# Attention on one core: the band mask added in PSUM by VectorE instead of by products on TensorE

## What is computed

```python
q, k, v = (layernorm(x) @ W.T + b for each of Wq, Wk, Wv)     # 16 heads of 32
scores = einsum("bhqd,bhkd->bhqk", q, k) * 32 ** -0.5
banned = (j >= 4) & (j < i - 128)                              # i: query, j: key
probs = softmax(where(banned, -inf, scores))
x = x + einsum("bhqk,bhkd->bhqd", probs, v) @ Wo.T + bo
```

## Time and profile before

| | us |
|---|---|
| median of 3 runs (lowest, highest) | 792.04 (791.56, 792.66) |
| span of the profiled execution, first to last instruction | 789.9 |
| PE busy in the span | 735.5 (93%) |
| DVE busy | 597.9 (76%) |
| ACT busy | 471.4 (60%) |
| POOL busy | 333.0 (42%) |
| mean granted TensorE clock | 0.976 |

### The profile page before, as it was taken

The page is one execution under the profiler, slowest core; times in us unless marked ns, Lnnn a source line. Parts: engine busy times, 40 slices in busy tenths (PEclk is TensorE's granted clock), DMA queues, the critical chain, the costliest instruction groups (busy, mean ns, idle before and its releaser), DMA issues. The chain is left out here.

```text
span 789.9 us, 14108 instructions
## 1 busy us (share of the span) xinstructions
PE 735.5 (93%) x5130; PEld 509.0 (64%) x5130; DVE 597.9 (76%) x1102; ACT 471.4 (60%) x1024; POOL 333.0 (42%) x330
## 2 busy tenths in 40 slices
PE   5988999999999999999987959999998999999984
PEld 4766777777777777777755747888874444444431
DVE  6886766886668866766677547887888999999982
ACT  5555766666667666766555214444455777667761
POOL 2011204213142134454373343445546667777662
PEclk9999999999999999999997979999999999999998
DMA  9200021304030331215330075455430233333231
GB/s 319 108 1 28 27 66 70 108 28 161 28 108 28 108 134 54 81 55 189 107 108 1 2 252 198 176 194 202 149 120 31 53 82 94 88 99 97 77 80 54
DMA packets 55218, 78.33 MB, mean 99 GB/s; under 512 B 36335, under 2 KB 38383, under 8 KB 53424
## 3 DMA queue, kind: packets, MB, share of 16 engines
q1 hardware_dynamic: 46336, 51.99, 20.2%
q0 software_dynamic: 8528, 24.93, 9.1%
q10 hardware_dynamic: 288, 0.52, 0.2%
HBM read 56.92 MB, written 17.59 MB: 94 GB/s over the span
## 5 line engine op out<-in xcount | busy, mean ns | idle before, releaser
L556 ACT ACTIVATE probs<-s_ps,neg_max 128x512 f32<-128x512 f32 (+2 forms) x256 | 152.3, 610 | 20.3 <-DVE neg_max L725 18.6
L725 DVE TENSOR_REDUCE neg_max<-s_ps 128x2 f32<-128x1024 f32 (+2 forms) x128 | 124.5, 1014 | 33.1 <-PE s_ps L963 32.6
L983 PE MATMUL pT_ps<-ident,probs 128*128 128x128 f32 x832 | 116.6, 282 | 9.3 <-DVE probs L746 8.3
L568 ACT ACTIVATE probs<-pT_ps 128x512 f32<-128x512 f32 x96 | 57.4, 598 | 98.6 <-PE pT_ps L983 97.8
L983 PEld LDWEIGHTS pT_ps<-ident,probs 128*128 128x128 f32 x832 | 95.0, 145 | 24.7 <-DVE probs L746 11.0
L746 DVE COPY probs<-pT_ps 128x512 f32<-128x512 f32 x112 | 76.8, 685 | 36.8 <-PE pT_ps L983 36.8
L1681 POOL TENSOR_TENSOR xg_own<-h,ln_w_sb 128x512 f32<-128x512 f32 x64 | 83.9, 1322 | 33.9 <-DVE h L1767 33.8
L896 PE MATMUL side_ps<-w_hi 128*128 128x512 f32 x172 | 71.1, 414 | 0.0
L420 POOL TENSOR_TENSOR aT_hi<-norm,one_col 128x512 fp32r<-128x512 f32 x15 | 15.6, 1040 | 125.4 <-DVE norm L737 87.1
L896 PE MATMUL side_ps<-w_hi,w_lo 128*128 128x512 f32 x172 | 67.5, 392 | 0.0
L896 PE MATMUL side_ps<-w_lo,w_hi 128*128 128x512 f32 x172 | 67.1, 390 | 0.0
(11 more groups left out here) (285 smaller groups left out, 1800.1 us busy)
## 6 DMA issues: line engine op xcount, KB each, us to landing
w_piece<-w_ffn SPq DMA_DIRECT2D x24, 512.0 KB, 3.5
w_stage<-w_ffn SPq DMA_DIRECT2D x12, 1024.0 KB, 4.8
xres<-x POOLq DMA_DIRECT2D x4, 1024.0 KB, 5.7
xn<-x SPq DMA_DIRECT2D x3, 1024.0 KB, 8.5
x<-xres POOLq DMA_DIRECT2D x3, 1024.0 KB, 4.8
xn<-c SPq DMA_DIRECT2D x2, 1024.0 KB, 6.1
v_next<-c SPq DMA_DIRECT2D x2, 1024.0 KB, 7.9
xn<-x SPq DMA_DIRECT2D x4, 256.0 KB, 3.5
```

The source lines that it names most:

```text
L556: nc.scalar.activation(weights[qt][:, h, at:at + width(qt)], s_ps[:, h, 0:width(qt)], ACT.Exp, bias=neg_max[:, qt % 2, h:h + 1], accum_out ...
L568: nc.scalar.activation(out, turned_p, ACT.Identity).then_inc(slot_copied[0], 1)
L725: nc.vector.tensor_reduce(neg_max[:, qt % 2, 2 * s:2 * s + 2], s_ps[:, 2 * s:2 * s + 2, 0:width(qt)], AX.X, ALU.max, negate=True).then_inc ...
L983: last = nc.tensor.transpose(pT_ps[:, k % 2, h * P:h * P + P], weights[qt][:, h, a:z], ident[:])
```

## The change

The four mask products of a masked unit are gone from PE. VectorE adds the same `window_mask` in place to the scores in PSUM, in one instruction for two heads (2 x 128 columns, or 2 x 124 for qt = 1), directly ahead of the maximum over these two heads, and waits for its own result (`masked_scores`) before it takes the maximum. `scores_ready` is now counted with the last score product of every second head, in all units. The clearing of `v_sinks` counts in `consts_ready` too, which now goes to 9; PE, the load of the sinks on SP, and VectorE ahead of its first maximum wait for 9.

```diff
--- before.py
+++ after.py
@@ -163,7 +163,7 @@
         rstd_ready, xn_ready = sem("rstd_ready"), sem("xn_ready")
         side_done, side_hi, side_left = sem("side_done"), sem("side_hi"), sem("side_left")
         sinks_gathered = sem("sinks_gathered")
-        v_sinks_cleared, v_sinks_loaded = sem("v_sinks_cleared"), sem("v_sinks_loaded")
+        v_sinks_loaded = sem("v_sinks_loaded")
         v_moved, c_split, rows_clipped = sem("v_moved"), sem("c_split"), sem("rows_clipped")
         c_loaded = [sem(f"c_loaded{n}") for n in range(EXPERTS)]
         piece_loaded, piece_done = sem("piece_loaded"), sem("piece_done")
@@ -171,6 +171,7 @@
         list_cleared, list_written, list_loaded = sem("list_cleared"), sem("list_written"), sem("list_loaded")
         dense_written, dense_loaded, x2_filled = sem("dense_written"), sem("dense_loaded"), sem("x2_filled")
         scores_ready, max_ready, exp_done = sem("scores_ready"), sem("max_ready"), sem("exp_done")
+        masked_scores = sem("masked_scores")
         slot_transposed, slot_copied = sem("slot_transposed"), [sem("slot_copied_act"), sem("slot_copied_dve")]
         heads_done, rinv_ready, rinv_widened = sem("heads_done"), sem("rinv_ready"), sem("rinv_widened")
         attn_ready, attn_hi_ready, attn_split = sem("attn_ready"), sem("attn_hi_ready"), sem("attn_split")
@@ -215,6 +216,9 @@
 
         def units_before(b, g, qt):
             return b * GU + g * TT + qt
+
+        def masks_before(b, g, qt):
+            return (b * HG + g) * (TT - 1) + qt - 1
 
 
 
@@ -349,7 +353,7 @@
                 load_piece(0, 0)
                 sp.wait_ge(side_left, nth(-1, "X3"))
                 load_x(1)
-                sp.wait_ge(v_sinks_cleared, 1)
+                sp.wait_ge(consts_ready, 9)
                 sp.wait_ge(side_left, nth(-1, "V0"))
                 place_sinks()
                 for b in range(BATCH - 1):
@@ -376,8 +380,8 @@
                 nc.gpsimd.memset(window_mask[:], 0.0).then_inc(consts_ready, 1)
                 nc.gpsimd.memset(minus_half[:], -0.5).then_inc(consts_ready, 1)
                 nc.gpsimd.memset(one_col[:], 1.0).then_inc(consts_ready, 1)
-                nc.gpsimd.memset(v_sinks[:], 0.0).then_inc(v_sinks_cleared, 1)
-                pool.wait_ge(consts_ready, 5)
+                nc.gpsimd.memset(v_sinks[:], 0.0).then_inc(consts_ready, 1)
+                pool.wait_ge(consts_ready, 6)
                 for t in (ident, ident_bf):
                     nc.gpsimd.affine_select(out=t[:], in_=t[:], compare_op=ALU.not_equal, fill=1.0, base=0,
                                             pattern=[[-1, P]], channel_multiplier=1).then_inc(consts_ready, 1)
@@ -722,6 +726,13 @@
 
                 def maxima(b, g, qt, s):
                     dve.wait_ge(scores_ready, units_before(b, g, qt) * 2 + s + 1)
+                    if blocks(qt)[2]:
+                        at = SINKS if qt == TT - 1 else 0
+                        free = SINKS if qt == 1 else 0
+                        scored = s_ps[:, 2 * s:2 * s + 2, at + free:at + P]
+                        nc.vector.tensor_tensor(scored, scored, window_mask[:, free:P].unsqueeze(1).to_broadcast([P, 2, P - free]),
+                                                ALU.add).then_inc(masked_scores, 1)
+                        dve.wait_ge(masked_scores, 2 * masks_before(b, g, qt) + s + 1)
                     nc.vector.tensor_reduce(neg_max[:, qt % 2, 2 * s:2 * s + 2], s_ps[:, 2 * s:2 * s + 2, 0:width(qt)],
                                             AX.X, ALU.max, negate=True).then_inc(max_ready, 1)
 
@@ -850,6 +861,7 @@
                     then(nc.vector.tensor_scalar(dense_row[:], dense[:], P - 1, None, ALU.bitwise_and))
                     then(nc.vector.scalar_tensor_tensor(dense_at[:], dense_row[:], float(TILES), dense_tile[:], ALU.mult, ALU.add))
 
+                dve.wait_ge(consts_ready, 9)
                 maxima(0, 0, 0, 0)
                 maxima(0, 0, 0, 1)
                 dve.wait_ge(wide_bias_loaded, 32)
@@ -943,7 +955,6 @@
                         project(name, side_ps[:], whole).then_inc(side_done, 1)
 
                 def scores(b, g, qt):
-                    sink, kts, masked = blocks(qt)
                     if qt == 0:
                         pe.wait_ge(side_left, keys_projected(b, g))
                     if units_before(b, g, qt):
@@ -953,16 +964,9 @@
                         for h in range(GH):
                             rows = slice(HD * h, HD * h + HD)
                             last = nc.tensor.matmul(s_ps[:, h, 0:width(qt)], q[rows, g % HG, cols], key_columns(k, rows, g % HG, qt),
-                                                    start=(n == 0), stop=(n == 2 and not masked), tile_position=(HD * h, 0))
-                    if not masked:
-                        last.then_inc(scores_ready, 2)
-                        return
-                    at = SINKS if qt == TT - 1 else 0
-                    free = SINKS if qt == 1 else 0
-                    for h in range(GH):
-                        last = nc.tensor.matmul(s_ps[:, h, at + free:at + P], ident_bf[:], window_mask[:, free:P], start=False, stop=True)
-                        if h % 2:
-                            last.then_inc(scores_ready, 1)
+                                                    start=(n == 0), stop=(n == 2), tile_position=(HD * h, 0))
+                            if n == 2 and h % 2:
+                                last.then_inc(scores_ready, 1)
 
                 def transpose_slot(b, g, qt, k):
                     slot = slots_of(qt)[k]
@@ -1044,7 +1048,7 @@
                     if name:
                         side(b, nth(b, name), name)
 
-                pe.wait_ge(consts_ready, 8)
+                pe.wait_ge(consts_ready, 9)
                 for t in range(TT):
                     pe.wait_ge(xn_ready, t + 1)
                     transpose_x(t, s_ps[:, t, :]).then_inc(side_done, 1)
```

## The result

The changed kernel takes 804.46 us (median of 4 runs, 802.55 to 806.96), the one before beside it 791.8 (786.52 to 792.66). The ratio is 1.019 (95%: 1.0158 to 1.0222), so some 15 us slower, with 12.5 to 17.6 as the interval (the two medians themselves lie 12.7 apart). The forecast was 8.5 slower, 800.5 us; the result lies inside the range of 795.2 to 807.5. Timed again (6 runs), it has the same ratio. So the sign was right and about two fifths of the loss were missing from the sum.

A forecast was written before the change was run, and what follows sets the result against it. PE was taken to bound most of attention, DVE its start and end; by unit classes 2.2 + 2.3 + 2.2 + 5.9 + 0.0 - 4.1 = +8.5 us, on the 792.0 median 800.5 us, range 795.2 to 807.5.

The forecast's parts named there:

- What bounds the kernel, and where the change bites: Attention: PE bounds most, DVE start and end; DVE's added work delays the slot 1 copy that PE awaits.
- The price of the addition: On DVE: 0.42 to 0.43 us per addition, 0.90 us per unit with waits, 43 us in all.
- 0.20 each: Rival, faster: DVE additions cost 0.20 us each, giving -4 us, 788 us; chance 0.07.
- 0.60 each: Rival, dearer addition: reading and writing PSUM in place costs 0.6 us each, +17 us, 809 us; chance 0.12.
- the one without a price for the wait: Rival: a dependent maximum on DVE starts without delay, a unit costs 0.70 us, +3.5 us, 795.5 us; chance 0.10.
- (a): Six units like (1,3,0), qt = 0, rounds 1 and 3: slot 3 waits for DVE's copy; 0.36 us each, +2.2.
- (c): Five units with statistics of x ahead of the copy, like (0,4,1): twice +0.6, three times +0.3, +2.2 us.
- (b): Three units like (1,2,0): PE's transposes of x wait for DVE's later sum for v; +0.76 us each, +2.3.
- (f): Seventeen units like (1,3,2), where the copy has slack: PE's saving counts in full, 17 x -0.24 = -4.1 us.
- (e): Nine units at about zero, such as those like (1,3,1) and (1,4,0), where other waits absorb PE's saving: 0.0 us.
- The clock: Rival: PE waits bring half speed mid-phase, 8 us of it giving 4 us too little work, 804 us; chance 0.13.
- (d): Eight units already bound by DVE, at attention's start and end: +0.7 to +0.9 us, one pair 0.9 together; +5.9 us.

The follow-up runs named there:

- The kernel without masks: Changed kernel with neither mask products nor additions, so banned keys keep their scores; 784.57 us, ratio 0.9929.
- the kernel before with POOL's new order: Kernel before, with POOL's load_residual of batches 1 to 3 put behind the widening of round 1's reciprocals; 789.21 us, ratio 1.0001.
- the kernel with 16 additions: Masks added by DVE in 16 units (qt = 2 or 3), PE products in the other 32; 788.09 us; with load_residual behind the widening 786.27 us, ratio 0.9969.
- the kernel with idle products: Changed kernel with 6 or 8 extra unread PE products in each of the nine units without side work; 805.46 us, ratio 1.0207.

## Why the prediction was right, and where its sum fell short

*What bounds the kernel, and where the change bites*: right. PE's share between 100 and 200 us fell to 95.8% (forecast 95), the waits for the slot 1 copies there rose to 6.2 us (forecast 5 or more), and they lie in the units named. The expert phase starts 16.7 us later (2.2 of it from ahead of the first unit), where 8 to 9 was named as the sign.

*The price of the addition*: right, 425 and 419 ns for 0.42 to 0.43, and 0.92 for a unit's two with their waits for 0.90. (The two maxima of the earlier trace rows last 1.22 and 1.21 us, so they do overlap by the 0.08 that the prediction took; with the 1.20 that it wrote it would be 0.05.) The two rivals that turned on it (0.20 each, 0.60 each) fall, and so does the one without a price for the wait. On that last one the Trainium skill (VectorE: DVE Perf Modes, The DRAIN you can't avoid) says, of eight copies in a row, that the semaphores between them cost nothing extra. The trace differs: here the addition runs 230.71 to 231.13 and its maximum starts at 231.17; that pair and the next take 0.46 and 0.45 us more than a maximum alone, not 0.35.

*Classes (a) to (c)*: right, 7.0 for 6.7. (a) and (b) are right to 0.1 us; in (c) the two units with qt = 1 took 0.71 more each where 0.6 was forecast.

*Class (f)*, "seventeen units that save in full", -4.1: the term that was too large. Twelve units save 0.17 to 0.20, not 0.24, the same for a narrow gap as for a wide one. Those like (1,2,2) save 0.06 to 0.09, because PE's transposes of x wait there for v (0.24 us in (1,2,2) of the changed kernel). (e) and (f) without (0,0,0) and (0,1,2) come to -2.5. The kernel without masks has the same figures, so they are PE's.

*(1,1,3) and (2,1,3)*, +0.69 and +0.66: the step that was missing. The prediction has no term for POOL's queue. Its widening was the last to come there already, by 0.2 us, as the kernel before with POOL's new order shows, so PE's saving was not to be had in these units; and in (1,1,3) POOL waits 0.46 us longer for the store than before. That is 1.35 us for the two units. In the kernel with 16 additions such a loss goes with the new order; in the changed kernel itself PE's wait for the widening is read from the trace, and its cure was not tried.

*The clock*, a rival with 0.13 and 8 us at half clock for 4 us of time: it came **beside** the forecast case and not in its place. 13.7 us of 35 to 400 us were at half clock, against 3.4 in the profile that I read; the products that ran in it cost 3.4 us by the kernel with idle products. It didn't come in the middle of the phase, from waits of 0.3 us, as that rival had it, but where PE already waited 2.6 us and now waits 2.7. And it isn't the change's alone: all three profiles of the changed kernel have the 13.7, but the kernel before, with 3.4 in its first profile and in the one with POOL's new order, shows 10.2 us in its second, with (0,0,3) 1.5 us longer. In that second pair batch 0's first units lose 4.0 us and not 5.9, and (3,2,0) to (3,3,1) lose 5.8 and not 3.3: from 400 to 455 us the kernel before stood at half clock for 6.8 us there and for 13.7 in its first profile, the changed one for 13.7 in both pairs. Attention as a whole grows by the same 15 us. So how much of the loss is the clock's can't be said from one pair. The Trainium skill (TensorE: Matmul & The Clock Gate, HAM oscillation) warns that idle gaps take the clock down repeatedly. The trace agrees for the units bound by DVE, where the clock fell twice from 60 to 72 us, and with the gaps filled none of the stretch from 35 to 400 us was at half clock.

The rest: (0,0,0) comes out 0.08 longer where 0.24 was to be saved, in the same stretch bound by DVE. Summed against 8.5: +2.9 for batch 0's first units with their half clock (1.6 in (d), 1.3 in (0,0,0), (0,1,2) and (0,0,3)), +1.35 for POOL's chain, +1.6 for savings that were booked too high, +0.3 in (c) and 0.1 in small ones: 14.8.

One more thing was mis-sized at the start. The profiled execution of before had 27 us at half clock between 400 and 480 us; another of its profiles shows 14. Its span of 789.9 is therefore no typical one: later medians were 788.0 to 790.4 us, and the median that belongs to this profile was 792.0. The forecast of 800.5, put on top of 792.0, stood 2 to 4 us too high on that account. That was luck: it hid part of the error, and a loss of 15 us lies only just inside the range, whose end is 15.5 above 792.0.

## What to carry to other kernels

Moving 0.2 us of work per step off the engine that binds pays only if the engine that takes it isn't the next to bind: here a saving of 0.17 to 0.20 us per unit was bought with 0.92 on an engine that hands back a copy in the middle of the unit. Go through the units one by one and move the work only in those with room (16 of 48 here, worth 0.3% together with POOL's new order), then look for the queue that becomes late because everything else is early. And read a phase's clock from more than one profile before a stretch at half clock enters a sum, or is blamed on a change.

## What the runs showed of the hardware

- An addition in place on a PSUM tile, with a bfloat16 operand from SBUF, costs DVE 694, 681, 425 and 419 ns for 512, 496, 256 and 248 elements per partition: 1.05 ns each and 156 ns fixed, the same as an addition of PSUM and float32 SBUF into SBUF. So the bfloat16 operand and the write to PSUM together change nothing; what each does alone no run shows.
- 32 products of one group took 1.87 us from start to start at 2.4 GHz and 3.57 at 1.2 GHz; the half clock from 71.5 us came behind 5 us (65 to 70) in which PE was busy for 2.04.
- Four mask products of 220 ns each cost PE 0.17 to 0.20 us together, as they overlap.
- Two DVE instructions that don't wait for each other overlap by 0.08 us; a maximum that waits for the addition in front of it starts 0.03 us behind its end.
